# Loading the ends of all edges in eleven parts, one per block of layer 2, and scattering the sorted groups without pauses

## The reference

```
# network 0, twice (layer 1: 64 -> 128, layer 2: 128 -> 128), then h @ W_out
agg = segment_sum(x[src], dst) / count          # mean over incoming edges
h   = relu(agg @ W_l + b_l + x @ W_r)
x   = layernorm(x + (h @ W_out + b_out))
# network 1, one message per edge
out = selu(concat(x[src], edge_attr) @ W1a + b1a) @ W1b + b1b
mean = segment_sum(out, dst) / count
x   = layernorm(x + (selu(concat(x, mean, u) @ W2a + b2a) @ W2b + b2b))
```

## Time and profile before

| | |
|---|---|
| median of 3 runs | 2644.59 us (2637.71 to 2650.03) |
| the profiled execution | 2639.33 us, its span 2637.6 us |
| busy share of the span | PE 80%, GpSimd (POOL) 69%, VectorE (DVE) 59%, ScalarE (ACT) 37% |
| mean granted TensorE clock | 0.878 of full speed |
| stage 3, from the first gather | 1142.85 to 2637.6 us |
| the blocks of layer 2 | about 696 to 1142 us |

### The profile page before, as it was taken

One profiled execution on the slowest core, in us unless ns is written; L12 is line 12 of the kernel. 1 busy time (PEld: TensorE's weight loads), 2 busy tenths in 40 slices (PEclk: granted clock), 3 DMA queues, 4 the chain that ended last, 5 costly groups with the idle time before them and its releaser, 6 DMA issues. The chain is left out here.

```text
span 2637.6 us, 52060 instructions
## 1 busy us (share of the span) xinstructions
PE 2112.2 (80%) x18382; PEld 1552.2 (59%) x18382; DVE 1552.7 (59%) x3098; ACT 986.8 (37%) x2255; POOL 1821.8 (69%) x1853
## 2 busy tenths in 40 slices
PE   1899999999969999946787877887877778766753
PEld 1555555555535555535676666666666666656753
DVE  6889999984435554554555555555555555543433
ACT  3777787780000000032333333333333333322322
POOL 5437766646655676777777777777777777777775
PEclk9999999999989999957988889889888988886665
DMA  8375787788696776434333333333333333332212
GB/s 291 125 228 201 207 252 238 208 235 225 220 188 208 231 231 228 141 94 117 74 71 69 70 64 79 66 68 77 68 68 74 72 67 74 66 67 51 52 42 45
DMA packets 478172, 346.45 MB, mean 131 GB/s; under 512 B 357844, under 2 KB 428687, under 8 KB 474253
## 3 DMA queue, kind: packets, MB, share of 16 engines
q1 hardware_dynamic: 367443, 272.49, 36.4%
q0 software_dynamic: 54240, 57.23, 10.0%
q10 hardware_dynamic: 56250, 13.52, 2.5%
HBM read 200.58 MB, written 142.39 MB: 130 GB/s over the span
## 5 line engine op out<-in xcount | busy, mean ns | idle before, releaser
L982 POOL DMA_INDIRECT A_sb<-source_terms,src_cur x1172 | 1119.9, 956 | 357.3 <-issue 350.9
L932 POOL DMA_INDIRECT sorted_edges<-pm_row,pm_to x440 | 482.5, 1097 | 199.3 <-issue 83.9
L1863 DVE TENSOR_TENSOR arena<-iota_code,arena 128x2048 f16<-128x2048 f16 (+1 forms) x392 | 438.1, 1186 | 27.7 <-PE cnt_ps L1410 25.3
L1077 ACT ACTIVATE A_sb<-cnt_ps 128x392 f32 (+1 forms) x784 | 383.7, 498 | 124.5 <-PE cnt_ps L1410 74.5
L1539 PE MATMUL agg_ps<-A_sb,arena 128*128 128x448 f16 x1911 | 379.3, 356 | 23.9 <-DMA A_sb<-counts_matrix 23.9
L2180 DVE TENSOR_TENSOR cnt_ps<-cnt_ps,A_sb 128x512 f32<-128x512 f32 x147 | 102.1, 694 | 444.8 <-DMA A_sb<-source_terms,src_cur 439.8
L1639 PE MATMUL agg_ps<-A_sb 128*65 128x48 f32 x2344 | 196.8, 245 | 180.4 <-DVE A_sb L2193 180.4
L1223 ACT ACTIVATE A_sb<-cnt_ps 128x512 f32<-128x512 f32 x147 | 87.4, 595 | 643.4 <-DVE cnt_ps L2180 643.2
L1410 PEld LDWEIGHTS cnt_ps<-arena 128*128 128x128 f16 x3136 | 190.0, 100 | 213.4 <-issue 164.3
L1410 PE MATMUL cnt_ps<-arena 128*128 128x98 f16 x3136 | 280.2, 214 | 32.9 <-ACT A_sb L1077 25.7
L1639 PEld LDWEIGHTS agg_ps<-A_sb 128*65 128x65 f32 x2344 | 182.7, 161 | 202.3 <-DVE A_sb L2193 197.2
(11 more groups left out here) (308 smaller groups left out, 3302.4 us busy)
## 6 DMA issues: line engine op xcount, KB each, us to landing
counts_matrix<-A_sb SPq DMA_DIRECT2D x14, 5488.0 KB, 17.3
A_sb<-counts_matrix SPq DMA_DIRECT2D x12, 5488.0 KB, 19.4
arena<-in_edge_attr_dram SPq DMA_DIRECT2D x96, 256.0 KB, 2.8
sorted_edges<-zrow SPq DMA_DIRECT2D x11, 1716.0 KB
A_sb<-source_terms,src_cur POOLq DMA_INDIRECT x1172
arena<-sorted_edges SPq DMA_DIRECT2D x143, 128.0 KB
overlapping_rows<-A_sb SPq DMA_DIRECT2D x1, 13056.0 KB, 39.4
A_sb<-in_edge_attr_dram SPq DMA_DIRECT2D x50, 256.0 KB, 2.8
```

The lines of the kernel that those rows point to most:

```text
L932: pool.indirect_dma_start(out=sorted_d, out_offset=bass.IndirectOffsetOnAxis(ap=pm_to[:, k, j:j + 1], axis=0), in_=pm_row[:, k, j, :], in_ ...
L982: pool.indirect_dma_start(out=gath[k][:, j * F:(j + 1) * F], out_offset=None, in_=p_d, in_offset=bass.IndirectOffsetOnAxis(ap=src_cur[k][: ...
L1077: act.activation(Asb(half)[:, :, bass.ds((b * BG + k) * GROUP, GROUP)].rearrange("p b (w j) -> p b w j", j=PAIR), cnt_ps[k % 2][:, 0:SUB * ...
L1863: ins = dve.tensor_tensor(hot_rows[:, slots], iota_code[:, 0:n, :].unsqueeze(1).to_broadcast([P, AT_ONCE * SUB // 2, n, 2]), turned[:, bas ...
```

## The change

The main part of the ends is cut into eleven parts (`END_PARTS = NSB - 3`) of 18 or 19 groups. `superblock2(s)` issues part s - 3, for source and destination, right behind the load of the matrix, for s = 3 to 13. The short remainders and `base_i` stay where they were, between `superblock2(2)` and `superblock2(3)`. The waits for `edges_in` go from 96 to 416 (`ENDS_IN`). The waits of the scatters on `pairs_begun`, and the semaphore, are gone.

```
+END_PARTS = NSB - 3
+ENDS_IN = 16 * 2 * (END_PARTS + 2)
...
             def superblock2(s, half, at_before=None):
                 sp.wait_ge(agg2_ready, s)
                 if s < NSB - 1:
                     sp.dma_start(A_sb[:, 1 - half, :], A_d[bass.ds(s - 1, 1), :, :].rearrange("a p n -> (a p) n")).then_inc(A_in[1 - half], 16)
+                if s >= NSB - END_PARTS:
+                    load_ends(s - (NSB - END_PARTS))
                 sp.wait_ge(x2_ready, s + 1)
...
+            def load_ends(part):
+                first, end = gE * part // END_PARTS, gE * (part + 1) // END_PARTS
+                for to, frm in ((src_e, src), (dst_e, dst)):
+                    sp.dma_start(to[:, first:end, :], frm[first * EG:end * EG].rearrange("(g p j) -> p g j", p=P, j=EJ)).then_inc(edges_in, 16)
+
             for to, frm in ((src_e, src), (dst_e, dst)):
-                sp.dma_start(to[:, 0:gE, :], frm[0:gE * EG].rearrange("(g p j) -> p g j", p=P, j=EJ)).then_inc(edges_in, 16)
                 sp.dma_start(to[0:TROWS_IN, gE, 0:TJ], frm[gE * EG:E - TREST].rearrange("(p j) -> p j", j=TJ)).then_inc(edges_in, 16)
...
                 for j in range(EJ):
-                    paired = q >= SOONER
-                    if paired and j % 2 == 0 and (q, j) != (SOONER, 0):
-                        pool.wait_ge(pairs_begun, (q - SOONER) * (EJ // 2) + j // 2)
                     pool.indirect_dma_start(
                         out=sorted_d, out_offset=bass.IndirectOffsetOnAxis(ap=pm_to[:, k, j:j + 1], axis=0),
-                        in_=pm_row[:, k, j, :], in_offset=None,
-                        engine_sem=pairs_begun if paired and j % 2 == 1 else None).then_inc(pm_gone[k], 16)
+                        in_=pm_row[:, k, j, :], in_offset=None).then_inc(pm_gone[k], 16)
```

More of the change, by code:

```diff
@@ L86 @@
 SLOT_AT = 32
+END_PARTS = NSB - 3
+ENDS_IN = 16 * 2 * (END_PARTS + 2)
 TOTALS = 4 * -(-NEG // 4)
-SORT_PAIRS = (PG - SOONER) * EJ // 2
 def cell_tiles(r):
@@ L460, in build @@
         gath_in = [sem(f"gath_in{i}") for i in range(DEEP)]
-        pairs_begun = sem("pairs_begun")
         (attr_turned, attr_moved, z_ready, z_made, selu_act, hot_made, msg_made, seg_ready, acc_added) = (sem(n) for n in (
@@ L519, in general_begins @@
             eng.wait_ge(pq_ready, NSB)
-            eng.wait_ge(edges_in, 96)
+            eng.wait_ge(edges_in, ENDS_IN)
         def general_ends(eng):
@@ L976, in _ @@
                 pool.memset(msg[k][:, :, F:F + 1], 1.0).then_inc(acc_zero, 1)
-            pool.wait_ge(edges_in, 96)
+            pool.wait_ge(edges_in, ENDS_IN)
             pool.wait_ge(p_stored, 16 * NSB)
@@ L1270, in fin_root @@
                 act.activation(st4[:, 2, cols, :], st4[:, 1, cols, :], ACT.Sqrt, bias=eps_t[0:CH, 0:1], scale=1.0 / F).then_inc(std4, 1)
-            act.wait_ge(edges_in, 96)
+            act.wait_ge(edges_in, ENDS_IN)
             for h in range(DEEP):
@@ L2136, in _ @@
             dve.wait_ge(base_in, 32)
-            dve.wait_ge(edges_in, 96)
+            dve.wait_ge(edges_in, ENDS_IN)
             step(dve.memset(ones_r, 1.0))
```

## The result

The changed kernel takes 2620.88 us (median of 4 runs, 2619.25 to 2622.42), the kernel before 2642.27 us beside it (4 runs, 2637.71 to 2650.03). The ratio is 0.9916 (95% interval 0.9897 to 0.9935): 0.84% faster. The profiled execution took 2619.25 us, its span 2617.5 us, at a mean granted clock of 0.880. Experiments 1 to 4, 7 and 8 were measured while the kernel before itself took 3316 and 3323 us, at a granted clock of 0.79; they are compared with those times alone. The ratios are those on record; the quotient of two medians can differ from them by up to 0.2%.

What follows compares the result with a forecast made beforehand. It took stage 3 as fixed by GpSimd's gathers and layer 2 as TensorE's; 2637.6 - 26.07 - 3.44 gave 2608.1 us of span, 2609.8 as a run, stated as 2614 leaning to the median, range 2605 to 2630.

Steps and rivals of the forecast that it cites:

- its rivals: Other outcomes: ScalarE's queue blocked or a leftover matrix stall, together 0.22; slower, 0.05; nothing changes, if stage 3 lengthens.
- The block of 59.09 us becomes one of 33.02: minus 26.07 us: Layer 2: with the ends no longer ahead of the matrix, its 23.94 us stall and the slow clock behind it go.
- Cost 0: Layer 2: each part's 3.3 us of transfers hides behind TensorE's block, within the matrix's slack of 12.6 us.
- in block 3 alone up to 3.5 us may be lost, once: Block 3's matrix goes out 3.9 us later, behind six short loads; possible loss 3.5 us, not taken into the sum.
- The rule of the Trainium skill: Transfers under 512 bytes miss the line rate, so cutting ends of 32-byte pieces only spreads the 36.7 us, saving nothing.
- Rival 1: Parts block ScalarE's DMA queue behind the matrix: 3 to 25 us back, 2618 to 2640; chance 0.22 shared with rival 2.
- scatters of group 3s + 11 behind a matrix: Layer 2: each such scatter takes turns with 44 KB matrix packets and costs ScalarE some 4 us.
- The pauses go: Layer 2: unpaused GpSimd needs 30.3 us a block instead of 32.7, so the 36.46 us block becomes 33.02: minus 3.44 us.
- with the stall gone and the pauses kept, the short stall would come sooner, and more than once: Layer 2: the 24 us stall had let GpSimd catch up with VectorE; removing the pauses must stand in for that.
- 4096 bytes a packet: Skill's packet limit: scatters would hardly wait beside a matrix, leaving 26.07 us of gain alone, 2611.5 us of span.
- Stage 3 is a fixed piece: Stage 3: GpSimd's gathers take 1494.75 us whatever precedes them, so the gain is how much earlier layer 2's last store comes.
- What would have shown it wrong: Signs: L1576 or L1582 waiting in many blocks, ScalarE issues of 3 to 8 us behind the ends, or longer stage 3.

Runs made afterwards that it cites:

- experiment 1: Changed kernel with the pauses of the scatters put back: 3307.9 us against 3316.45 for the kernel before, ratio 0.9989.
- experiment 2: Kernel before without the `pairs_begun` waits, ends whole at their old place: 3350.58 us, ratio 1.012 to the kernel before.
- experiment 3: Changed kernel with its six short DMAs issued in the last block: 3341.15 us, ratio 1.0091 to the kernel before.
- experiment 4: Changed kernel with each part of the ends ahead of the block's matrix load: 3342.24 us, ratio 1.0089 to the kernel before.
- experiment 7: Repeat of the changed kernel with the pauses put back: 3313.69 us against 3322.76 for the kernel before, ratio 0.9975.
- experiment 8: Repeat of the kernel before with only the pauses removed: 3347.58 us against 3322.76, ratio 1.0097.
- the second pair: Kernel before and changed kernel, both unchanged, measured again: 2639.28 and 2620.54 us, ratio 0.9924.
- experiment 9: Changed kernel with the ends in three parts, in blocks 3 to 5, pauses kept: 2622.34 us against 2644.33 for the kernel before, ratio 0.9913.
- experiment 11: Changed kernel with the pauses put back, eleven parts, run a third time: 2623.24 us against 2644.33 for the kernel before, ratio 0.9915.
- experiment 12: Changed kernel with four parts in blocks 4 to 7, short loads in the last block, pauses kept: 2623.64 us against 2643.94 for the kernel before, ratio 0.9912.
- experiment 10: Changed kernel with all eleven parts in a row at the old place, pauses kept: 2650.48 us (one run) against 2644.33 for the kernel before.
- experiment 5: The kernel before, unchanged, timed again with a profile: 2639.28 us (11 runs).
- experiment 6: The changed kernel, unchanged, timed again: 2620.54 us, ratio 0.9924 to the kernel before.

## Why the prediction came out as it did

The forecast was 29.5 us of gain in the span, and 2614 us. Measured were 2620.88 us: inside the range of 2605 to 2630, but just above the 2606 to 2620 that had 0.70, where the forecast put its rivals. The medians differ by 21.4 us and, in the second pair, by 18.7. The first pair of traces has 27.95 us of gain in layer 2, the second 24.55; 7.0 and 7.8 us are lost ahead of layer 2, some 0.85 in stage 3.

That layer 2 came within 1.6 us of 29.5 in the first pair is partly luck. Blocks 3 and 4 together gave 22.0 us (22.2 in the second pair), the later short stalls 3.6 (2.2), and 2.8 (0.4) came from the block at 658.55, which stands ahead of the blocks that the forecast cut out and has no term in it.

*"The block of 59.09 us becomes one of 33.02: minus 26.07 us".* Right in mechanism, and shown: with the ends at their old place in eleven parts the stall is 26.30 us, with the parts behind the matrices no matmul waits for one (experiments 9, 11 and 12). Cut at its first matmul that block, 58.89 before, became 36.62, and block 3 ahead of it 33.50.

*"Cost 0" for the parts, and "in block 3 alone up to 3.5 us may be lost, once".* The parts of blocks 5 to 12 do cost nothing, each block is at 33.02 us. That cutting saves no transfer time held as well: in experiment 10 the 22 loads and the short one behind them kept SyncE's queue from 739.76 to 778.90, 39.1 us, where the whole ones kept it 36.7 by the same measure (35.2 in experiment 5). The rule of the Trainium skill (DMA: Bandwidth & Descriptors, Specifications) that speaks against loads of 32-byte pieces agrees with the trace: 1.65 MB of ends in 36.7 us are 45 GB/s, where a matrix of 5.6 MB lands in 18.4 us (305 GB/s). The slack paid for it. Block 3 costs 0.48 us itself and 3.60 in the block behind it, 4.1 together (3.7 in experiment 6), so this term was known and then left out of the sum. Rival 1's mechanism is there too, ScalarE's DMA held 11.87 us, but it cost 0.23 us. The 3.60 came by the other way that the prediction names, scatters of group 3s + 11 behind a matrix. Which part of the group's lag comes of the matrix that left 3.35 us late, and which of the ends behind it, is not shown.

*"The pauses go": minus 3.44 us.* Right in sign and mechanism in layer 2, with the addition that "with the stall gone and the pauses kept, the short stall would come sooner, and more than once": experiment 11 has three blocks of 35.34, 37.44 and 34.28 us. Its layer 2 takes 462.2 us (666.39 to 1128.59), those of the changed kernel 456.35 and 457.73 (667.00 to 1124.73): 4.5 to 5.9 us, and 3.7 to 4.2 without their first block, for the pauses. The stall of 3.44 us itself varies: in experiment 5 the kernel before has 1.7 and 0.5 us in its place. In the medians the difference is 2 to 3 us (2623.24 against 2620.88 and 2620.54, not measured side by side), less than the intervals can tell. Where TensorE's matmuls came in bursts, the same edit cost 1.0 to 1.2%; nothing in the prediction allowed for that, and no row of the trace of before shows it.

The chain behind it, a scatter that takes turns with packets of a matrix, is borne out so far as it goes: the matrix still travels in packets of 44 KB (DMA queues of the changed kernel, 742 to 746 us),

```profile
q1 hardware_dynamic: 34, 1.49, 86.8%
q0 software_dynamic: 24, 0.03, 2.3%
```

and three scatters of group 23 behind the matrix of 768.06 landed up to 13.6 us behind the last one's issue, where the prediction's 4 us each make 12. With the waits on own scatters gone, no stall is left at the old place. The Trainium skill's 4096 bytes a packet (DMA: Bandwidth & Descriptors, SWDGE vs HWDGE vs iDMA), which the page gives as preferable and the prediction read as a bound, is not what this load does; the measurement decides.

*"Stage 3 is a fixed piece".* Right: 1494.75 and 1495.60 us; 1495.2 and 1496.1 in experiments 5 and 6.

*The step that failed*, within a forecast that held, is the silent one, that the time up to layer 2 stays what it was. The sum took 658.55 us over unchanged; it became 665.55. Of the 7.8 us in the second pair, 4.3 are the clock: stretches at its lower level that fall elsewhere against the same work, one on a block, one behind a wait instead of ahead of it. Another 2.3 are 0.2 to 0.25 us a block, at full clock, in every kernel with eleven or four parts and in none with whole ends or three, whichever pauses it has. Why loads that are issued hundreds of microseconds later should do this stays open: it is the same with eight loads as with 22, and the pauses don't set it. Six loads don't have it, so a limit between six and eight is not ruled out, nor is something else in the compiled program, and no row names a cause.

*What would have shown it wrong* did in part: ScalarE's queue was held behind a matrix and its ends for 11.87 us in block 3, 9.95 in block 5 and 3.2 to 4.0 in two more. Only the first cost TensorE anything, 0.23 us. Such holds are no proof against the ends: the kernel before has one of 7.94 us at 1030.49, where no ends are in flight.

## What to carry to other kernels

Look at what stands ahead of the load that is waited for, not at how much is loaded: the same 36.7 us of transfers cost 26 us at one place in the queue and 4 at another, and three parts do it as well as eleven. An engine that issues DMAs between its own instructions passes on to them every hold of its queue and every landing that its loads wait for. So ask of each moved load which other queue's next issue falls behind it, and read which of the two an issue waited for: here the hold of 11.87 us cost 0.23, and the landing of one group 3.6. And a gain of under 1% should be summed over all stages of two traces of each kernel, because a kernel whose timing shifts by a few microseconds gets its slow-clock stretches at other places, to its loss (the last block of stage 1) or to its credit (the block at 665.55).

## What the runs showed of the hardware

- The recorded times of matmuls can run ahead of TensorE's work: in experiment 2 a semaphore rose 11.5 us behind the recorded end of the matmuls that raise it, beside a granted clock of 0.97, against 0.01 to 0.02 us in the changed kernel at 2620 us. A gap in such a row is not rest. The same kernel took 2644 us at one time and 3316 us at another on the chip numbered 11 in both results, at a mean clock of 0.88 and 0.79. So the chip alone doesn't set it, though some expectations speak of "the other chip".
- In that condition GpSimd's scatters without pauses, the same work at a closer spacing, made the kernel 1.0 to 1.2% slower in four comparisons (2 and 8 with the kernel before, 3 and 4 with 1); whether they draw on the same limit as the matmuls was not shown.
- The same 3.4 us at half clock cost nothing ahead of a wait and 1.7 us behind it (experiments 5 and 6).
- SyncE's second DMA behind a 5488 KB load took 17.23 us to issue. ScalarE's third in the same stretch took 11.87 us (11.5 to 12.3 in block 3 of four traces with the short loads ahead of that matrix and ends behind it, those of the changed kernel and of experiments 6, 9 and 11). In experiment 12, which has neither in block 3 and came to this DMA 14.2 us behind the matrix, it took 1.55 us. Holds of 9.3 to 9.95 us came in block 5 of most of them, and one of 7.94 us in the kernel before with no ends about, so what sets their length stays open.
